# New timetables and new PSUM banks for one recurrent two-layer mixer kernel on one core

## The reference, cut

```python
# x: (16, 512, 128).  ln = layernorm, no weights
# layer 0
h = ln(x)
att = softmax((h_head @ w_att_val[head]) @ h_head.T / sqrt(8))      # 16 heads of 8, all 512 keys
m   = concat_heads(att @ v_head) @ out_w.T + out_b                 # v = h @ wv_w.T + wv_b
e   = argmax(h @ Wg + bg)                                           # one of 8 experts per token
f   = gelu(h @ W1[e]) @ W2[e]                                       # 128 -> 512 -> 128
x1  = x + m * silu(f)
# layer 1
h = ln(x1)
local  = softmax over a window of 32 back, 16 heads of 8            # q, k, v = h @ wq, wk, wv
remote = softmax over 64 latents (k, v pooled over 8 tokens), 8 heads of 8, then @ r_out_w
m = (sigmoid(q . gate_local) * local + sigmoid(q . gate_remote) * remote) @ w_out
f = h
for layer in 2:                                                     # 8 heads of 64, window 64
    q, k, v = shift_token(f) @ wqkv[layer]
    q, k = rotary_xpos(l2norm(q) * q_scale, l2norm(k) * k_scale)
    f = f + local_attention(q, k, v) @ wo[layer]
    n = ln(shift_token(f));  a, g = split(n @ w1[layer] + b1[layer])
    f = f + (a * gelu(g)) @ w2[layer] + b2[layer]
out = x1 + m * silu(f)
```

## Time and profile before

| what | value |
|---|---|
| median of 3 runs | 3463.22 us (3461.16 to 3474.72) |
| the profiled execution's own time | 3440.83 us |
| span of the profile | 3439.0 us, 83502 instructions |
| TensorE busy | 3112.3 us, 90% |
| TensorE weight loads | 1889.5 us, 55% |
| VectorE busy | 2466.9 us, 72% |
| ScalarE busy | 2338.7 us, 68% |
| GpSimd busy | 1261.4 us, 37% |
| mean duration of `max_b` (L1752), of L1756, of `nmax_f` (L2063) on VectorE | 0.68, 0.69, 0.68 us |

### The profile page before, as it was taken

How to read it: one execution, slowest core, us unless ns; L and a number is a source line. 1 busy time by engine, 2 the same in 40 slices (tenths; PEclk the granted TensorE clock), 3 DMA queues, 4 the chain that set the end, 5 groups by cost and what they waited for, 6 DMA issues and landing times.

```text
span 3439.0 us, 83502 instructions
## 1 busy us (share of the span) xinstructions
PE 3112.3 (90%) x34007; PEld 1889.5 (55%) x34008; DVE 2466.9 (72%) x5000; ACT 2338.7 (68%) x4758; POOL 1261.4 (37%) x799
## 2 busy tenths in 40 slices
PE   5589799999999999999999999999999999999976
PEld 5168445556564646555565656565555656464644
DVE  6432487868687877878676868778786868687643
ACT  1265467777777786777767776867777777778744
POOL 1622034333333443444333333444443333344343
PEclk9889899999999999999999999999999999999987
DMA  6256110101011111101011111111010101111000
GB/s 190 69 160 187 48 28 14 32 27 38 27 28 31 34 31 34 31 16 33 23 36 29 28 31 34 31 34 31 15 35 22 38 27 28 34 31 31 5 13 4
DMA packets 130458, 138.95 MB, mean 40 GB/s; under 512 B 17972, under 2 KB 112542, under 8 KB 129566
## 3 DMA queue, kind: packets, MB, share of 16 engines
q1 hardware_dynamic: 120368, 104.77, 11.2%
q0 software_dynamic: 9712, 28.85, 2.9%
HBM read 80.87 MB, written 35.39 MB: 34 GB/s over the span
## 4 chain that ended last, share of the span: by engine, by line
PE 46%; DVE 21%; ACT 9%; POOL 6%; issue 4%; DMA 2%; SPq 2%; POOLq 0%; ACTq 0%; DVEq 0%
PE bank L1882 5%; PE bank L1319 4%; DVE turn_f L2056 4%; PE bank L698 4%; PE bank L1926 3%; ACT prob_a L1388 3%; PE bank L1303 3%; PE bank L1332 3%; DVE nmax_a L1443 3%; PE bank L1868 3%; PE bank L1858 2%; PE bank L1849 2%; DVE ss L2049 2%; DVE nmax_f L2063 2%; POOL turn_f L1797 2%
## 5 line engine op out<-in xcount | busy, mean ns | idle before, releaser
L1388 ACT ACTIVATE prob_a<-bank 128x512 f32<-128x512 f32 x1024 | 564.4, 607 | 190.0 <-PE bank L1332 185.2
L1443 DVE TENSOR_REDUCE nmax_a<-bank 128x1 f32<-128x512 f32 x768 | 502.5, 684 | 161.6 <-PE bank L1303 160.5
L1791 POOL TENSOR_TENSOR rn<-ss,minus_half 128x16 f32<-128x16 f32 x128 | 377.8, 2952 | 270.6 <-DVE ss L2051 268.6
L1814 POOL TENSOR_TENSOR rs_f<-rs_f,minus_half 128x4 f32<-128x4 f32 x32 | 32.6, 1018 | 1108.2 <-DVE rs_f L1181 1108.2
L1797 POOL TENSOR_TENSOR turn_f<-turn_f 128x512 f32<-128x512 f32 x256 | 324.3, 1287 | 207.7 <-DVE turn_f L2056 207.7
L1332 PE MATMUL bank<-Qst_a,Kst_a 74*128 74x512 bf16 x1024 | 378.9, 389 | 18.9 <-ACT prob_a L1388 9.5
L1944 ACT ACTIVATE area<-bank 128x512 f32<-128x512 f32 x640 | 349.9, 603 | 63.2 <-PE bank L1882 55.2
L2056 DVE TENSOR_TENSOR turn_f<-area,rotf 128x1024 f32<-128x1024 f32 x256 | 307.6, 1219 | 8.7 <-POOL area L1801 6.2
L1303 PE MATMUL bank<-Kst_a,Qst_a 72*128 72x512 bf16 x768 | 302.2, 394 | 5.4 <-DMA Kst_a<-dk_a 1.2
L1319 PE MATMUL bank<-prob_a,V_a 128*9 128x512 f32 x2048 | 274.5, 609 | 13.2 <-ACT prob_a L1388 11.8
L1801 POOL TENSOR_TENSOR area<-turn_f,rn 128x1024 f32<-128x1024 f32 x128 | 267.5, 2090 | 19.0 <-POOL turn_f L1797 0.9
(11 more groups left out here) (288 smaller groups left out, 7007.4 us busy)
## 6 DMA issues: line engine op xcount, KB each, us to landing
Qst_a<-dq_a SPq DMA_DIRECT2D x192, 96.0 KB
Kst_a<-dk_a SPq DMA_DIRECT2D x192, 96.0 KB
dq_a<-prob_a SPq DMA_DIRECT2D x80, 128.0 KB
dk_a<-prob_a SPq DMA_DIRECT2D x48, 128.0 KB
area<-xs_d SPq DMA_DIRECT2D x39, 128.0 KB, 4.3
ys_d<-otok_f SPq DMA_DIRECT2D x39, 128.0 KB, 1.9
x_a<-in_x_in SPq DMA_DIRECT2D x16, 256.0 KB, 2.8
xs_d<-turn_f SPq DMA_DIRECT2D x4, 1024.0 KB, 9.9
```

What stands on the lines that cost most here:

```text
L1388: nc.scalar.activation(dst, bk.full(act, product)[0:rows, :], func, **kw).then_inc(a_emptied["act"], 1)
L1443: nc.vector.tensor_reduce(out=nmax_a[:, g, t, j:j + 1], in_=bk.full(dve, f)[:], op=ALU.max, axis=AX.X, negate=True).then_inc(emptied, 1)
L1791: nc.gpsimd.tensor_tensor(rn[:, t % 2], ss[:, t % 2], minus_half[:], ALU.pow).then_inc(f_root, 1)
```

## The change

The numbers that set the order are replaced: STEP goes from 177.9173333 to 180.9273333, and every table in `TIMES` and every string in `SEATS` is another. Nothing else is changed: no instruction, no helper and not the opening. The new planned times were made with a rule that VectorE and GpSimd hold a common SBUF port one at a time.

```diff
-STEP = 177.9173333
+STEP = 180.9273333
 TIMES = {
         "sync": {
             "b": ((1.3, 2.3),
-                  (-13.62627, -12.62627)),
+                  (35.96565, 36.96565)),
...
         "gpsimd": {
             "gate": ((0, 1),
-                     (-47.04021, -46.04021)),
+                     (-60.17119, -59.17119)),
...
 SEATS = {
...
-    "b": "331035134113500030533454325534522200",
+    "b": "453142034115500154332154355200244140",
```

More of the change, by code:

```diff
@@ L231 @@
             "b": ((1.3, 2.3),
-                  (-13.62627, -12.62627)),
+                  (35.96565, 36.96565)),
             "head": ((0, 9.5, 12, 17, 29.6),
-                     (-15.12171, 8.59514, 10.05181, 18.6592, 69.16135)),
+                     (-5.06008, 21.218, 34.84341, 42.50965, 50.21754)),
             "f": ((0, 8.1, 14.2),
-                  (-76.6243, -60.87516, -48.15163)),
+                  (-124.7127, -124.7107, -54.16294)),
             "a": ((14, 34, 36, 56, 59, 83),
-                  (-117.93683, -108.734, -106.94609, -81.78519, -71.29696, -27.93752)),
+                  (-91.89826, -81.91236, -66.99357, -66.99157, -55.3079, -49.04586)),
             "finish": ((14.7, 15.7),
-                       (-39.45796, -38.45796))},
+                       (-45.66689, -44.66689))},
         "gpsimd": {
             "gate": ((0, 1),
-                     (-47.04021, -46.04021)),
+                     (-60.17119, -59.17119)),
             "b": ((0.5, 1.5),
-                  (-4.97401, -3.97401)),
+                  (-8.35954, -7.35954)),
             "head": ((1, 2),
[1 row of a table removed]
[1 row of a table added]
             "f": ((5, 6.5, 10.4, 11.9, 15.8, 17.3, 21.2, 22.7, 47, 70, 71.5, 75.4, 76.9, 80.8, 82.3, 86.2, 87.7),
[2 rows of a table removed]
[2 rows of a table added]
             "feed": ((6.8, 7.8),
-                     (-115.0227, -114.0227))},
+                     (-114.05328, -113.05328))},
         "tensor": {
@@ L357 @@
                    96.4, 97.6, 98.8, 100, 101.2, 102.4, 104.6, 108),
[10 rows of a table removed]
[10 rows of a table added]
             "feed": ((6.175, 8.3, 8.55, 9.05, 9.55),
-                     (-119.82581, -107.55224, -103.59258, -103.40648, -101.00127)),
+                     (-121.05039, -109.01918, -107.35539, -103.65502, -103.65302)),
             "finish": ((11.2, 12.2),
-                       (-93.02697, -92.02697))},
+                       (-96.27779, -95.27779))},
         "vector": {
             "gate": ((113, 113.2, 113.4),
[1 row of a table removed]
[1 row of a table added]
             "b": ((0, 0.2, 0.5, 1.5, 2.6, 3, 3.2, 3.5, 5.1, 5.2, 5.3, 5.35, 7.1, 7.2, 7.3, 7.35, 9.1, 9.2, 9.3,
@@ L404 @@
                    98.4, 99.6, 100.8, 102, 103.5, 105, 111),
[10 rows of a table removed]
[10 rows of a table added]
             "feed": ((6.55, 6.8, 7.1, 8.8, 9.3, 9.8, 10.725),
-                     (-113.68945, -113.49199, -109.75291, -99.7432, -99.7412, -97.62405, -91.88652)),
+                     (-116.70738, -116.70538, -112.98853, -106.41422, -105.95242, -103.43652, -99.56629)),
             "finish": ((13.2, 13.4, 13.6),
-                       (-76.74182, -61.91878, -61.91678))}}
+                       (-81.48863, -52.9393, -39.30843))}}
 SEATS = {
-    "a": ("254203542054321052043524034510511415123514045345035030102525035230214135243515300531031003"
-          "4513421403035420250352105113200"),
-    "b": "331035134113500030533454325534522200",
-    "head": "54501230315415320432",
-    "f": ("150451305243052304031214124341450420024254245301445324051152302420342030532035420311432412"
-          "4311412041201312"),
-    "feed": "033345204"}
+    "a": ("054203542054041534521235041235511435123514040335045130150325032530334130243010355031031003"
+          "4150321035142054530342401430105"),
+    "b": "453142034115500154332154355200244140",
+    "head": "41335530125215024350",
+    "f": ("102121540243052104031214034241452412524251405253252023450230142042505025320503520413452412"
+          "4531012040134013"),
+    "feed": "333325423"}
 B_AT = 5
```

4 lines of the change are left out of this document (2 added, 2 removed), and 202 rows, old and new, of the table TIMES.

## The result

The changed kernel takes 3494.98 us (median of 5 runs, 3492.23 to 3503.52) against 3473.99 for the kernel before (5 runs): ratio 1.0071, 95% interval 1.0046 to 1.0097. The forecast was 3430, faster. The time lies above the range, and the sign is wrong.

A forecast was written before the change was run, and what follows sets the result against it. The prediction took TensorE's own work plus small waits to bound the kernel. Gains of 1.2 + 0.7 + 0.1 = 2.0 us a row, times 15, plus 3 for the stacks, took 3463.2 to 3430 us; range 3398 to 3482.

The forecast's parts named there:

- The bound: A quiet row of 186.7 us is TensorE's own 177.46 us of work plus small waits; the whole room is 9.2 us.
- Busy time unchanged at 177.5: Sign to check: TensorE's busy time in a quiet row stays 177.5 us, with idle time near 7.2 us.
- The forecast's quiet row, 184.7: Predicted length in us of a row at full clock after the change, against 186.7 before.
- The split: Second mixer, q and k split on VectorE: fewer port collisions shorten TensorE's waits by 1.2 us a row (0.1 to 2.0).
- The gather: Feed-forward's first layer: four GpSimd issues moved behind tile 3 let tile 2 start earlier, gaining 0.7 us a row (0.3 to 1.2).
- A new wait of over 1 us: Sign the prediction is wrong: such a wait newly standing in TensorE's timeline in the second mixer.
- `pool_b`: L1706 moved behind its tile's second L2056, meeting a GpSimd instruction in its middle: gain 0.1 us a row (0 to 0.4).
- the stacks: TensorE's first L1291 of a head stage waits less for its stack's DMA: 3 us over the whole run (0 to 7.6).
- SyncE: Two `hT` transfers moved behind the first six stack loads, with 18.5 us in which to land: no effect.
- Seats: Nearly every product gets another of six banks; argued to even out: nothing, within 0.5 us a row either way.
- The sum without the gather: The summed gain was 33 us: 2.0 us a row times 15, plus 3 for the stacks; the gather gave 0.7 a row.
- The collisions rival: Second mixer on VectorE: L1722, L2051 and L1197 collide with GpSimd, 1.7 us a row more, 3488 us; chance 0.15.

The follow-up runs named there:

- experiment 1: The changed kernel with the gather's copy and four issues back between tiles 1 and 2 on GpSimd: 3436.89 us, ratio 0.9912 to the kernel before.
- experiment 10: The kernel before with only three steps of the head's split (L1191, L1193, L1197) moved on VectorE: 3452.05 us, ratio 0.9956.
- experiment 4: The changed kernel with the gather moved behind the root of the layer's normalisation on GpSimd: 3432.95 us, ratio 0.9897.
- experiment 5: The changed kernel with the gather between tiles 2 and 3 of the first layer on GpSimd: 3405.71 us, ratio 0.9905.
- experiment 2: The kernel before with the gather alone moved behind tile 3 of the first layer on GpSimd: ratio 1.0014.
- experiment 6: The changed kernel, gather still behind tile 3, with the last group's six stack loads cut to 3 rows of 24 each: 3405.5 us (one run).
- experiment 11: The changed kernel with the gather halved: copy and two issues between tiles 1 and 2, two issues behind tile 3: 3439.07 us (one run).
- experiment 12: The kernel of experiment 1 with the old bank strings: 3519.16 us (one run).
- experiments 5 to 8: Runs on the short-opening chip: experiment 5, experiment 6, and experiment 1's kernel with 12 small ScalarE copies (3409.11 us) or with VectorE's old timetable (ratio 1.0226).

## Why the prediction was wrong, point by point

**The bound.** Right: TensorE's own work and small waits, and gains came from the waits. "Busy time unchanged at 177.5" was off: it is 178.5 in experiment 1's quiet row of 185.5. The instructions are the same there. A likely reason is how the profile counts: the products shown above have a length of 0.60 us each and start 0.43 us apart, so a short wait behind one vanishes in its length. The forecast's quiet row, 184.7, was 0.8 us too low for the lists without the collision.

**The split, 1.2 us a row.** Right, mechanism and size: experiment 10 gives 1.4 in a quiet row and 0.44% of the run (0.21 to 0.67) by itself. There TensorE's waits of 1.09 and 0.49 us are gone and one of 0.17 for GpSimd's `area` has become 0.92. L1193 went as worked out, L1195 came better than said (0.82 against 1.15), and L1197 won the tie in every row (1246 ns at most), where the rival needed it lost.

**The gather, a gain of 0.7 us. This is the step that failed.** I took the four issues as 6 us of GpSimd time and asked only who waits for GpSimd. TensorE's waits for L1801 did go, from 29.5 us (39 times) in the whole run to 13.4 (4 times), but not by this move: with the gather back in its old place (experiment 1) they are 13.4 us too, and three places of the gather make no odds (experiments 1, 4, 5). So the term itself is worth nothing in the new lists, and in the old ones its gain didn't show either (experiment 2). Each issue also starts a transfer. Its row on GpSimd is 0.95 us long, but in the kernel before a gather lands 2.4 to 4.4 us after its issue:

```profile
DMA to landing us min/median/max: 2.4/2.6/4.4
```

The Trainium skill, page "Perfetto Trace Analysis", section "DMA Instruction — SWDGE (GPSIMD)", says the same of such a row: it ends when the descriptors are generated, not when the data has moved. By that rule, and by the row above, the stretch to look for neighbours in was not the 6 us on GpSimd but up to the last landing; I wrote "behind tile 3 the issues are hidden" and never laid SyncE's queue beside it. Of SyncE's queue I looked at `hT` alone. A new wait of over 1 us was named as a sign of being wrong, but for the second mixer; it came 140 us into the row.

The price, from experiment 1 to the changed kernel: in a row at full clock 185.5 to 187.9 us, and all 2.4 of them arise at this one place (idle time of 0.3 and 1.7 us, the rest hidden in lengths). On average with the clock it is 185.97 to 190.66: 4.7 us a row, 66 us over the fourteen of the profiled executions, where the sum had a gain of 10.

**The clock.** The sum had no term for it. The forecast was made from rows in which it fell now and then (30.7 us of low clock), and treated that as given. A wait of 1.7 us at a fixed place in each row made it fall in 12 of 14. The same goes the other way: without the gather's wait and with the small waits of the second mixer shortened it falls in none (experiments 1, 4, 5, 6, 11), and that is part of why they gain 2.6 us a row on average but 1.2 in a quiet row. In the kernel before, four of the falls begin about where the wait of 0.88 us in the second mixer ends (25.4 to 26.0 us into the row), two behind waits of 1.6 us, and the longest, 10.2 us, behind one of 2.33. So the low clock in the earlier trace rows had waits of its own in the trace. By the 3.2 us that 6.8 us at 1.2 GHz cost, those 30.7 us were worth about 1 us a row (an estimate).

**`pool_b`, the stacks, SyncE.** TensorE's wait of 0.44 us for `pool_b` is gone, but the first transposes after the row's turn wait 0.69 instead of 0.43. With the small waits beside them the turn is 0.3 us shorter, where I took 0.1. The waits for stack loads ahead of L1291 (7.6 us) are gone, and those ahead of L1303 rose from 1.2 to 3.5: net 5.3, where I took 3. No wait for `hT` shows.

**Seats.** Said to be nothing by argument, and not tested by anything in the trace; experiment 12 shows that they can be worth 6.3 us a row if they don't fit the order. What new strings with a new order are worth against old with old, no run separates.

**The sum without the gather** is 33 - 10 = 23 us, or 0.7%; experiment 1 measures 0.9% (0.7 to 1.1), and experiment 4 1.0%. That they lie this close is in part luck: the rows gain 2.65 us each, 37 over the fourteen, where the sum has some 1.5, and about 1 us of the 2.65 is clock; against it stand 4.4 us more behind the last start of L1483, for which the sum had no term either. The collisions rival named 3488, which the time lies near, but for another collision at another place: none of its three mechanisms happened.

## What to carry to other kernels

An instruction that starts a DMA is two things that move, its slot and its transfer; lay the transfer beside every other queue's transfers before calling the move hidden. Where a reader starts long after the producer's end with nothing before it, look for what else was on the wires, not for a dependency. And price a new wait on TensorE of about 2 us twice, once for itself and once for the clock that may fall behind it; here even 0.88 us had a fall behind it in four rows of fourteen.

## What the runs showed of the hardware

TensorE's semaphore increments were seen up to 2.7 us late (one of another counter 3.1) while a gather issued by GpSimd and six stack loads issued by SyncE moved data together, up to 1.1 us late with half of the gather, and the readers started in time when the two moved one after the other (experiments 1, 4, 5) or the loads were small (experiment 6, on the other chip). ScalarE's increment for L1405 in the same stretch was in time; of other increments there, VectorE's for L2068 and L2071 and in eight rows ScalarE's for L1388, the trace has none. The Trainium skill, page "SBUF — State Buffer", section "Who interferes with whom", says that TensorE and ScalarE never wait on anyone, and that DMA does not contend with a compute engine. For the matmuls themselves nothing here contradicts that: it is the news of them that is late. Whether only TensorE's is held, and why, is open, and so is whether the recording of the trace has a part in it. For that speaks that increments are missing from the traces with the long opening, beside gathers and loads (of the counter of TensorE's attention products 2808 in the changed kernel and 2767 in experiment 1) and none from those of experiments 5 to 8 (2834 in each). No run here can tell it.

A wait of TensorE of 0.45 us at this place did not lower the clock in any row, one of 1.7 lowered it in 12 of 14, one of 2.3 in 11 of 14. The length alone doesn't decide it: in the kernel before the clock fell behind 0.88 us of waiting in four rows, and neither there nor in the changed kernel did it ever fall behind the 1.3 to 1.4 us at the row's turn. When it fell for 6.8 us the row was 3.2 us longer.
